# First attention of a two-layer kernel: f16 halves of the exponentials turned by DMA, division moved behind the values' product, steps laid out anew

## The reference, cut to what matters

```python
q = (layernorm(x) @ wq.T + bq).reshape(B, Tq, 16, 32).transpose(0, 2, 1, 3)
k, v = ...                                   # the same from the context, 154 keys
scores = jnp.clip(q @ k.T * scale, -100.0, 100.0)
scores = jnp.where(mask == 0, -jnp.inf, scores)
attn = softmax(scores)                       # over 154 keys
x = x + tanh(g) * ((attn @ v) @ wo.T + bo)
```

## Time and profile before

| | us |
|---|---|
| median of 3 runs (2787.85 to 2791.42) | 2790.43 |
| the profiled execution: its time | 2809.87 |
| the profiled execution: its span | 2808.1 |
| first clip of the first attention to the first matmul of the next stage | 41.22 to 471.64 |
| clips of units 0, 8, 56 and 63 | 41.22, 100.04, 397.09, 436.44 |
| one block of the steady part | 49.5 |

### The profile page before, as it was taken

How to read it: one execution, slowest core, us unless ns; L and a number is a source line. 1 busy time by engine, 2 the same in 40 slices (tenths; PEclk the granted TensorE clock), 3 DMA queues, 4 the chain that set the end, 5 groups by cost and what they waited for, 6 DMA issues and landing times. The chain is left out here.

```text
span 2808.1 us, 44981 instructions
## 1 busy us (share of the span) xinstructions
PE 2644.7 (94%) x16990; PEld 1473.8 (52%) x16990; DVE 1594.4 (57%) x2629; ACT 1425.9 (51%) x3586; POOL 1042.0 (37%) x823
## 2 busy tenths in 40 slices
PE   5999988999999989999999979999999999999999
PEld 3554544444444457777777645565444444444444
DVE  6888885655555346655656568988543422333222
ACT  3888885323222146666666548999443222322221
POOL 1455451465555636666766500111102201221111
PEclk8999999999999999999999989999999999999999
DMA  6221214222222269999999842321420110011000
GB/s 186 52 85 57 74 31 169 61 61 61 75 70 54 76 215 289 285 296 282 288 288 289 207 101 76 91 44 42 157 64 16 46 42 34 16 46 46 19 12 30
DMA packets 287479, 311.17 MB, mean 111 GB/s; under 512 B 155169, under 2 KB 164129, under 8 KB 287265
## 3 DMA queue, kind: packets, MB, share of 16 engines
q1 hardware_dynamic: 250400, 240.96, 27.0%
q0 software_dynamic: 36864, 67.34, 11.7%
HBM read 198.86 MB, written 75.89 MB: 98 GB/s over the span
## 5 line engine op out<-in xcount | busy, mean ns | idle before, releaser
L1376 POOL DMA_INDIRECT ids<-sh_tk,sh_su x256 | 269.8, 1054 | 243.9 <-PE sh_gu L55 70.5
L55 PE MATMUL ex_gu<-ex_xT,ex_h 128*128 128x256 f16 x3072 | 347.5, 273 | 4.6 <-issue 3.8
L55 PEld LDWEIGHTS ex_gu<-ex_xT,ex_h 128*128 128x128 f16 x3072 | 301.2, 98 | 53.9 <-issue 4.4
L1775 POOL DMA_INDIRECT xp<-ex_oo,ex_to x128 | 242.3, 1893 | 178.6 <-ACT ex_oo L1683 123.2
L2323 POOL TENSOR_TENSOR fe_prodT<-fe_pp,fe_prodT 128x512 f16<-128x512 f32 x64 | 77.5, 1210 | 591.2 <-ACT fe_prodT L2108 591.2
L521 PE MATMUL at_g<-id,at_p 128*128 128x128 f32 x1280 | 205.1, 288 | 38.7 <-POOL at_p L901 30.7
L1510 DVE SCALAR_TENSOR_TENSOR ex_h<-ring,ex_h 128x1024 f16<-128x1024 f32 x128 | 151.1, 1222 | 153.0 <-ACT ex_h L1500 153.0
L521 PEld LDWEIGHTS at_g<-id,at_p 128*128 128x128 f32 x1280 | 164.9, 169 | 106.9 <-issue 41.7
L680 ACT ACTIVATE at_s<-at_s,at_mx 128x154 f32<-128x154 f32 x512 | 210.4, 417 | 0.0
L900 POOL TENSOR_TENSOR at_p<-at_s,at_rs 128x1024 f32<-128x1024 f32 x64 | 121.5, 1898 | 223.3 <-DVE at_rs L800 223.3
L55 PE MATMUL at_g<-hm_zT,hm_w 128*128 128x512 f16 x768 | 182.1, 389 | 19.8 <-issue 12.5
(11 more groups left out here) (331 smaller groups left out, 5407.8 us busy)
## 6 DMA issues: line engine op xcount, KB each, us to landing
ring<-L_ffn_expert_gate_up_w SPq DMA_DIRECT2D x64, 1024.0 KB
ring<-L_ffn_expert_down_w SPq DMA_DIRECT2D x64, 512.0 KB
ring<-x SPq DMA_DIRECT2D x24, 1024.0 KB, 5.8
x<-ring SPq DMA_DIRECT2D x16, 1024.0 KB, 4.7
zrows<-hm_zs SPq DMA_DIRECT2D x32, 256.0 KB
xp<-ring SPq DMA_DIRECT2D x8, 1024.0 KB
out<-ring SPq DMA_DIRECT2D x8, 1024.0 KB, 4.3
ring<-xp SPq DMA_DIRECT2D x7, 1024.0 KB, 5.7
```

The lines of the kernel that those rows point to most:

```text
L55: mm = nc.tensor.matmul(out, lhs(a, k), rhs(b, k), start=start and i == 0 and j == 0, stop=stop and i == n - 1 and j == 2)
L1376: e.indirect_dma_start(ids, bass.IndirectOffsetOnAxis(slotu[b % 2][:, t, j:j + 1], 0), pair[b % 2][:, t, j, :], None, bounds_check=SLOTS - ...
L1775: e.indirect_dma_start(dst, bass.IndirectOffsetOnAxis(to[:, n:n + 1], 0), o32[y % 2][:, t, :], None, bounds_check=T + SLOTS - 1, oob_is_er ...
```

## The change

`attention` is parted in `first_attention` and `second_attention`; the second is the old code for layer 1, with semaphores of its own. In the first:

- ACT's exponentials no longer add up sums. They are split in f16 halves: the high half is a copy, on ACT for even units and on DVE for odd ones (`high`), the low half a subtraction on POOL. POOL no longer multiplies by reciprocals.
- One transposing DMA for each unit takes `prob` (2 halves x 1280 columns of f16) to `pT` (`turn_keys`), in place of the 10 transposes on PE and the three copies out of PSUM. `high` waits for the DMA of the unit two before.
- The values are held as f16 halves too. `values` makes the product in three terms (`o`, 12 narrow and 3 wide matmuls) and the sums of the exponentials by products with ones (`d`, 8 narrow and 2 wide); both take a bank. ACT forms the reciprocal as exp(-ln(sum)), DVE multiplies in the next step (`divide`), ACT copies the high half, and POOL subtracts the low half one step later (`halve`).
- `low` moves from DVE to POOL. `finish` comes at 15, 16, 17, 18 steps after the block's first, where it was at 13, 13, 14, 14; projections at -5 to -2 (before -7 to -4); `oT` is double. Three more steps are run at the end.

```diff
+def first_attention(nc, K, A, dst, sync_ahead, rows_ahead):
...
+    STEPS = UNITS + UPB + 3
...
+    NS = 3
+    NP = 2
...
+        V = [sb(f"V{g}", [P, 2, D], F16) for g in range(BATCH)]
+        VR = [sb(f"VR{g}", [P, 2, KT, P], F16) for g in range(BATCH)]
...
+        prob = [sb(f"p{i}", [P, 2, HH * (P + HD)], F16) for i in range(NP)]
+        pT = [sb(f"pT{i}", [P, 2, HH + 2, BLK], F16) for i in range(2)]
...
+        each, every = sb("each", [P, HD], F16), sb("every", [P, P], F16)
+        recip, o32 = [wv[:, i, :] for i in range(2)], [wv[:, i + 2, :] for i in range(2)]
+        wo, oT = A.homes.b, [A.homes.a, sb("oT1", [P, 2, KT, BLK], F16)]
...
+        VALS, FIN = (7, 8, 11, 12), (15, 16, 17, 18)
+        Z, LOW = (-14, -14, -10, -10), (-13, -13, -9, -9)
...
+            else:
+                at(n - 20, "load", b, 0)
+                for i, m in enumerate((15, 14) if b == 2 else (17, 15)):
+                    at(n - m, "stats", b, i)
+                for t in range(TPB):
+                    at(n + (Z[t] if 2 < b < NB else max(Z[t], -12)), "prepare", b, t)
+                    at(n + (LOW[t] if 2 < b < NB else max(LOW[t], -11)), "low", b, t)
+                    at(n - 8, "turn", b, t)
+                proj = (-5, -4, -3, -2)
...
                 at(n + proj[m], "project", b, m)
...
+                what = divmod(i, 2)
+                at(n + m, "values", b, what)
+                at(n + m + 1, "divide", b, what)
+                at(n + m + 2, "halve", b, what)
             for t in range(TPB):
                 at(n + FIN[t], "finish", b, t)
-        for i, m in enumerate((1, 2) if maps_ahead else ()):
...
+            plan[UNITS + 5].append(("split_ahead", 0, i))
...
-            def keys_turned(i, j0, part):
-
-                out = bank(("p", i, part), left(i, part))
-                n = min(4, HH + 2 - j0)
-                for j in range(n):
-                    mm = e.transpose(out[:, j * P:(j + 1) * P], keys_of(prob[i % NP], j0 + j), K.id32[:, :])
-                mm.then_inc(s["p_mm"], 1)
...
+                    for i in range(unit - NP, unit):
+                        e.wait_ge(*keys_landed(i))
+                    out = bank(("o", n), (s["o_div"], n + 1))
...
+                    heads = [(slice(j * HD, (j + 1) * HD), place(gi * HG + j)) for j in range(HG)]
+                    for hv, hp in TERMS:
+                        for rows, k in heads:
+                            o = grp * P + rows.start
+                            e.matmul(out[rows, :], V[g][:, hv, o:o + HD], ptb[:, hp, k, :],
+                                     start=(hv, hp) == TERMS[0], stop=False)
+                    for hv, hp in TERMS:
+                        mm = e.matmul(out[:, :], VR[g][:, hv, grp, :], ptb[:, hp, HH + gi, :], start=False,
+                                      stop=(hv, hp) == TERMS[-1])
+                    mm.then_inc(s["o_mm"], 1)
+                    out = bank(("d", n), (s["d_ln"], n + 1))
+                    for hp in range(2):
+                        for rows, k in heads:
+                            e.matmul(out[rows, :], each[:, :], ptb[:, hp, k, :], start=hp == 0, stop=False)
+                    for hp in range(2):
+                        mm = e.matmul(out[:, :], every[:, :], ptb[:, hp, HH + gi, :], start=False, stop=hp == 1)
+                    mm.then_inc(s["d_mm"], 1)
...
+                        e.wait_ge(s["o_lo"], 4 * B + 4)
...
+                    e.activation(recip[n % 2], bank_of["d", n][:, :], ACT.Ln).then_inc(s["d_ln"], 1)
+                    e.wait_ge(s["d_ln"], n + 1)
+                    e.activation(recip[n % 2], recip[n % 2], ACT.Exp, scale=-1.0).then_inc(s["d_inv"], 1)
...
+                    e.wait_ge(s["o_div"], n + 1)
+                    e.copy(oT[B % 2][:, 0, 2 * u + gi, :], o32[n % 2]).then_inc(s["o_hi"], 1)
...
+                    x = e.activation(to, to, ACT.Exp, bias=mx[i % 3][:, k:k + 1])
...
+            def high(i):
+
+                if not 0 <= i < UNITS or i % 2:
...
+                e.wait_ge(s["expd"], 2 * i + 2)
+                if i >= NP:
+                    e.wait_ge(*keys_landed(i - NP))
...
+                e.copy(first_keys(prob[0][:, 0, :]), sc[i % NS][:, :, 0:P])
+                e.copy(last_keys(prob[0][:, 0, :]), rest_of(i)).then_inc(s["p_hi0"], 1)
...
+                    exps(n - 1, part)
+                high(n - 1)
+                for what in plan[n]:
                     piece(*what)
...
                 elif what == "low":
-                    nm.vector_low(n)
+                    if B == 0:
+                        nm.vector_low(n)
...
+                    if n >= 2:
+                        e.wait_ge(s["o_hi"], n - 1)
+                        e.wait_ge(s["o_lo"], n - 1)
+                    e.wait_ge(s["o_mm"], n + 1)
+                    e.wait_ge(s["d_inv"], n + 1)
+                    e.tensor_tensor(o32[n % 2], bank_of["o", n][:, :], recip[n % 2], ALU.mult).then_inc(s["o_div"], 1)
...
+                e.tensor_copy(first_keys(prob[1][:, 0, :]), sc[i % NS][:, :, 0:P])
+                e.tensor_copy(last_keys(prob[1][:, 0, :]), rest_of(i)).then_inc(s["p_hi1"], 1)
...
+            for n in range(STEPS):
+                for what in plan[n]:
+                    if what[0] == "prepare":
+                        piece(*what)
+                if n < UNITS:
...
+                    if i >= NS:
+                        e.wait_ge(s["p_lo"], i - NS + 1)
...
+                    e.wait_ge(s["clip"], i + 1)
+                    for part in range(2):
+                        half = slice(HG * part, HG * part + HG)
+                        e.tensor_reduce(mx[i % 3][:, half], sc[i % NS][:, half, :],
+                                        AX.X, ALU.max, negate=True).then_inc(s["neg"], 1)
+                for what in plan[n]:
+                    if what[0] == "divide":
+                        piece(*what)
+                high(n - 1)
+                for what in plan[n]:
+                    if what[0] not in ("prepare", "divide"):
+                        piece(*what)
...
+                elif what == "low" and B:
+                    nm, _, n = whose(B, k)
+                    nm.low(e, n)
+                elif what == "halve":
+                    u, gi = k
+                    n = 4 * B + 2 * u + gi
+                    e.wait_ge(s["o_hi"], n + 1)
+                    e.tensor_tensor(oT[B % 2][:, 1, 2 * u + gi, :], o32[n % 2], oT[B % 2][:, 0, 2 * u + gi, :], ALU.subtract
+                                    ).then_inc(s["o_lo"], 1)
...
+                for what in plan[n]:
+                    if what[0] == "low":
+                        piece(*what)
+                if 0 <= n - 1 < UNITS:
+                    i = n - 1
+                    rows = prob[i % NP]
+                    e.wait_ge(s[f"p_hi{i % 2}"], i // 2 + 1)
+                    e.tensor_tensor(first_keys(rows[:, 1, :]), sc[i % NS][:, :, 0:P], first_keys(rows[:, 0, :]), ALU.subtract)
+                    e.tensor_tensor(last_keys(rows[:, 1, :]), rest_of(i), last_keys(rows[:, 0, :]), ALU.subtract
+                                    ).then_inc(s["p_lo"], 1)
+                for what in plan[n]:
+                    if what[0] != "low":
+                        piece(*what)
...
+                e.dma_start_transpose(pT[i // TPB % 2][:, :, :, t * P:(t + 1) * P].rearrange("p h j n -> p (h j) n"),
+                                      prob[i % NP][:, :, :].rearrange("p h n -> p (h n)")
+                                      ).then_inc(s[f"keys{i % NP}"], 16)
...
+            for n in range(STEPS):
+                late = [what for what in plan[n] if what[0] in ("finish", "limits")]
+                for what in plan[n]:
+                    if what not in late:
+                        piece(*what)
+                if 0 <= n - 1 < UNITS:
+                    turn_keys(n - 1)
+                for what in late:
+                    piece(*what)
```

More of the change, by code:

```diff
@@ L398, in attention @@
[L398 to L414, removed]
+        sc = [sb(f"s{i}", [P, HH, CTX], F32) for i in range(NS)]
@@ L444, in attention @@
-            if b:
-                at(n + (-10 if b == 1 else turns[0]) - 12, "load", b, 0)
-            if L0 and b < NB:
-                for i, m in enumerate((8, 7, 7)):
-                    at(n - m, "limits", b, i)
-            early = 2 if b == 1 else 3 if L0 or b == 2 else 4
-            if b:
-                for i in range(2 if L0 else 3):
-                    at(max(n + turns[0] - early - (2 if L0 or b < 3 else 4) + i, 0), "stats", b, i)
-            for t in range(TPB):
-                for lead, what in ((-early, "prepare"), (1 - early, "low"), (-1, "turn")):
-                    if b:
-                        at(n + turns[t] + lead, what, b, t)
-                if L0 and b < NB:
-                    at(n + t, "bias", b, t)
+                for i in range(2):
+                    at(-1, "stats", 0, i)
@@ new lines, in first_attention @@
+                for t in range(0, TPB, 2):
```

(20 more changed lines are left out.)

734 lines of the change are left out of this document (460 added, 274 removed).

## The result

The changed kernel takes 2847.36 us (median of four runs, 2846.70 to 2848.54) against 2790.57 us: a ratio of 1.0206, 95% interval 1.0188 to 1.0223. It is slower, as forecast, but by 57 us where 17 were forecast, and outside the range. The profiled execution took 2847.82 us with a span of 2846.1.

A forecast was written before the change was run, and what follows sets the result against it. PE is busy nearly all the time, but no engine is full in an attention block, so waits inside positions decide. Blocks -7.5 us plus clock drops 24.5 make +17 on 2790.4: 2807 us, own range 2796 to 2822, with rivals 2768 to 2828.

The forecast's parts named there:

- The engines' sums: Busy time per attention block after the change: PE about 34 us, DVE 38 to 40, ACT about 37, POOL 36; all under 49.5.
- (c): Rival, values products on PE: narrow f16 products do not run side by side, 18 us more, 2825 us; chance 0.07.
- The chain inside a position: Waits between engines in a steady block's eight positions, p0 to p7: they sum to 49.4 us, 0.1 under now.
- The clock: PE's clock drops at p4 and p7 of each block, 1.75 us each: 3.5 x 7 blocks = 24.5 us.
- Other blocks: Attention blocks outside the steady ones: block 0 at 0, block 1 -4.0 us, block 7 with the end -3, before the clock.
- Block 0: First attention block: DVE's values splitting and a queued second pair of row turns against savings, taken as 0, 6 both ways.
- Block 1: Second attention block: no finish in p0 to p2, so -4.0 us against now.
- Block 7 and the end: Last block about 33 us for 39.4, the end behind it about 39 for 35.2: -3 us, before the clock.
- (a): Rival: no clock drops, as PE's idle stretches are shorter; -7.5 us, 2783 to 2793; chance 0.20.
- (d): Rival: a clock drop at every wait, also p0 and before p3; one 1.75 more a block, +12, 2819 us; chance 0.06.
- (b): Rival: POOL's `halve` of p6 comes early, so p7 is DVE's 4.8 us and the block 46.4; 2768 us; chance 0.25.

The follow-up runs named there:

- e10: Changed kernel with split later, turns earlier, product earlier, POOL's low half first, z later, and key DMA turning high halves alone: 2748.58 us, ratio 0.9855.
- e8: Changed kernel with DVE normalising the rows (z) behind the clip and maxima of its step instead of ahead: 2833.30 us, ratio 1.0176.
- e6: Changed kernel with 11 more f16 matmuls at each of three PE waits (positions 0, 4, 7) from block 1 on: 2830.66 us, ratio 1.0177.
- e2: Changed kernel with block 1's second pair of row turns issued in step 3 with the first pair: 2835.46 us, ratio 1.0188.
- e1: Changed kernel with the next stage's weight split one step later, behind ACT's last high half: 2836.03 us, ratio 1.0188.
- e11: Changed kernel with its key DMA turning the high halves alone, 1280 columns instead of 2560: 2842.43 us, ratio 1.0190.
- e4: Changed kernel with POOL's `halve` ahead of the keys' subtraction of the same step: 2821.64 us, ratio 1.0145.
- e3: Changed kernel with DVE's product of a values group in the step of its matmuls, not one later: 2808.54 us, ratio 1.0091.

## Why the prediction was wrong

*The engines' sums* held but for PE's, 38.0 us a block at full clock (e10) for 34. (DVE's terms as I gave them add up to 36.4 to 38.6 and not to 38 to 40; 40.3 measured.) Narrow f16 products run side by side (twelve in 0.83 us), so (c) falls; exponentials run at a pitch of 0.33 (eight in 2.6 us), the key DMA is issued in 3.1 and lands after 5.0 us, POOL's subtraction takes 2.6.

*The chain inside a position* held in its mechanism and nearly in its sizes, without drops of the clock (position 1 is measured with the z that I had put into 2, and 5 with that of 6, so these are added up):

| | p0 | p1+p2 | p3 | p4 | p5+p6 | p7 | block |
|---|---|---|---|---|---|---|---|
| forecast | 8.2 | 11.55 | 4.8 | 8.2 | 8.85 | 7.8 | 49.4 |
| measured | 8.16 | 11.67 | 4.83 | 8.16 | 10.47 | 8.57 | 51.9 |

Two terms were too small. At p5+p6 I priced POOL's neighbourhood at 0.2 us; it is 1.9, z at 2.91 for 1.00 (e8). GPSIMD Engine Reference, in the Trainium skill, says in its Key points that POOL shares its SBUF interfaces with VectorE, and contends with its 2-port modes and its operations with two SBUF inputs. The trace shows such a contention: z and the limits are stretched while clip (1.43) and maxima (1.50) are not; in which mode VectorE ran them it does not show. At p7 I had `finish` held by `halve` until 4.3 us (3.9 measured), but sent PE straight to the scores: DVE's own product of that finish and its statistics, 0.75 and 1.28, stand ahead of the next clip.

*The clock* was right, and 0.6 us a block too dear. In blocks 1 to 6 positions 0, 4 and 7 are 17.2 us over their lengths without a drop, at 1.7 each, in ten or eleven places: 2.9 a block, for 3.5. TensorE: Matmul & The Clock Gate, section HAM oscillation, in the Trainium skill describes such a fall in each turn of a loop with long waits; here it came in ten or eleven of the eighteen waits at these positions, and e6 takes most of it away by filling them. (The two falls that I read at 57.5 and 1589.3 lie at 57.1 and 1589.7; nothing hangs on it.)

*Other blocks* is the step that failed, with 24 of the 35 us by which the attention's +52.2 exceeds +17. Block 0: "I take 0, with 6 both ways", measured +8.4. The wait of the second pair of turns was named, but priced without the queue's length ahead of it, 12 us of all engines, of which e2 takes 10.2 away. Block 1: forecast -4.0 and 3.5 for the clock, measured +3.7. Its saving of finishes is there (position 0 is 5.58), but it leaves PE idle for 7.1 us and brings the longest drop of blocks 1 to 6, 10 us, which I had not counted: the scores and the values group run at the lower clock (twelve narrow products 1.47 us for 0.83), and position 3, 6.74 for 4.83, waits for PE's scores. There is also a z beside POOL in position 1 (2.13 us), but e8, which moves it, leaves block 1 at 53.1; no run takes the drop of block 1 away. Block 7 and the end: forecast -3 and 3.5, measured +12.3. ACT's in-order queue with `split_ahead` ahead of the last copy, 6.4 us (e1), was not looked at. Units that come faster there than a key buffer turns round wait 2.6 to 3.8 us each for their DMA; a shorter DMA (e11) takes 2.1 us off block 7 and nothing off the end. The other 3 us or so stay open. The steady blocks 2 to 6 account for 11 us, 9 of them by the two terms above less the clock.

The rivals: (a) and (d) fall by the drops at about two places a block. That "slower" came true is no proof of the sum: the steady blocks bear out most of it, and the rest of the loss comes from the places that I had put at nothing or at a gain. (b) was a real way out, not taken by the change itself: `halve` stood behind the subtraction, and e4 is that rival, made. It gives 20 us.

## What to carry to other kernels

Follow a moved step in the first and the last pass of a loop with the same care as in the steady one: every in-order queue there holds other things, here a weight split on ACT, and a key turn, a mask and a load on SP, worth 17 us between them at their places. When work is moved from an engine to DMA, count the DMA engines as an engine, with their share times the period: 12 us a block became 44, and that is the floor of any better order that keeps these transfers. In a table that ties all engines to the same steps, ask of every bank in which step it is freed: moving that one operation up (e3) was worth 29 us.

## What was not expected of the hardware

- DVE's one-input f32 operation on 2 x 512 columns takes 1.00 us alone, 2.91 beside a two-input operation of POOL (changed kernel, block 3); DVE's clip and maxima beside such operations are not lengthened (1.43 and 1.50 us). In that place and in e10 (257.12, 2.25 us) it ends about 1.00 us behind the end of POOL's instruction.
- A transposing DMA of 2560 f16 columns lands after 5.0 us (4.9 to 10.0), one of 1280 after 3.5 (e10). The engines' share of a block falls from 0.93 of 47.7 us to 0.71 of 43.4, that is 44 to 31 us, about 12 of which are other transfers.
- Taking a wait away often moved or added clock drops elsewhere, so that e1 and e2 gave back about half of their gain and e8 9.4 of 11 us in blocks 1 to 6; with most waits gone (e10) blocks 2 to 5 ran at 1.00 throughout.
